# A graph block and a ConvLSTM on one NeuronCore: the scan's x terms partly from memory with shifted taps, 128-row products only, and another place for the load of y

## The chip, the cores and the metric

One NeuronCore of a Trainium2 chip. The metric is the device time of one execution in microseconds (us), the median of three runs. The core has TensorE (PE; its weight loads PEld), VectorE (DVE), ScalarE (ACT), GpSimd (POOL) and SyncE (SP), which issues nearly all DMA transfers here and does them in program order, as every engine does its own list.

## The reference

x is (16, 48, 32, 32). Two blocks follow each other, in float32:

```
# block 1: graph convolution in windows of 8 x 8 nodes
y    = affine(conv1x1(x, fc1))                       # 48 channels
idx  = top_k(-dist(normalized nodes), 9)             # 9 nearest of 64 nodes
feat = [x_i, x_j - x_i];  h = max_k gelu(affine(feat @ ew.T + eb))
x1   = affine(conv1x1(h, fc2)) + x
# block 2: ConvLSTM over the 32 rows of x1, forward and backward, 3 taps along the row
gates = conv1d(concat[x1_row, h], w_mid, 3 taps) + b  # i, f, g, o: 4 x 48 channels
c = sigmoid(f) * c + sigmoid(i) * tanh(g);  h = sigmoid(o) * tanh(c)
y = w_proj @ [h_fwd, h_bwd];  out = relu(batchnorm(y)) + x1
```

## The kernel before, in words

**Graph stage.** The 32 groups (a row of windows of two images, 512 nodes) are worked off in turns 0 to 31, a software pipeline: in turn g, PE gathers the edges of group g with one-hot matrices (line 632), ACT takes the gelu (L849), DVE the maximum over the neighbours (L1242), while DVE makes the one-hot matrices of group g+1 (L1227) from the spread indices `ib` and finds the neighbours of group g+3 (L1210, L1218). Each engine has its own `turn(j, b)`. SP's turn issues, in an order written out by hand: the load of y of group g+3 (`load_y`, L297), the x for the residual (`load_xres`), the store of the indices of group g+3 (`store_idx`, L323), the store of x1, the keys of group g+5 (`load_keys`, L306), and the spread of the indices to 64 partitions each (`spread_idx`, L332), which first waits until the store has landed. From turn 14 on a turn also loads one block of the scan's weights (`load_scan_weight`, L401) and a piece of a mask (`load_rest`, L406). Groups 0 to 7 give rows 0 to 7 of x1, groups 8 to 15 rows 24 to 31, then rows 16 to 23 and 8 to 15. POOL and ACT write x1 to `xh` as two float32r parts: the low part to partitions 0 to 47, the high part to 64 to 111.

**Scan.** 32 steps; in each the forward direction d = 0 (row s), then the backward one d = 1 (row 31−s). A product is taken as high·high + high·low + low·high. Per half-step PE adds 18 products of 512 columns into two PSUM banks (m = 0: gates i and f; m = 1: g and o), three taps each:

- `x_part` (L703): six over `xh`, 128 rows: x low, x high, and in the gaps (partitions 48 to 63 and 112 to 127) two sixteens of x high once more, for the low part of the weights. Copies inside SBUF put them there (`load_twins`, L413).
- `h_part`, first six (L718): 48 rows each, h high in `ht` for m = 0 and in `he` for m = 1, with the low weights `w_e`. These wait for `h_top` (POOL's copy of h, L1119) and `h_edge` (ACT's copy, L920).
- `h_part`, last six (L724): 128 rows of `ht`: h high, a row of ones, h low, and the third sixteen of x high. They wait for `h_lo` (POOL's subtraction, L1121) and for `x_third`, a copy that SP may issue only when the gates of the step before are done (`load_third`, L422).

Then ACT takes two tanh (L904, L910), DVE makes the cell and h (L1335, L1343, L1346, L1353) with a tanh of ACT between (L914), and POOL and ACT write h back in parts. SP stores h to memory (`store_h`, L461), loads x1 for the residual (`load_x1r`), and from step 17 on the h of both directions for the projection, two products on PE per step (`project`, L735). SP, PE, DVE, ACT and POOL run steps in loops: PE, ACT and DVE steps 2 to 13 as two rounds of six steps, SP and POOL most of their steps.

Of the kernel before, what the change touches and what calls it, by code (L numbers as in the profile page):

```python
# [22 lines left out]
P = 128  # L23
# [31 lines left out]
def build(nc, xs, xrow, w1, ones_sel, col1, jcol, wedge, edge_scale, edge_shift, ident9, w2, col2,  # L55
# [5 lines left out]
    x1_d = nc.dram_tensor("x1_d", [H, C, B, W], F32, kind="Internal").ap()  # L61
    hist_d = nc.dram_tensor("hist_d", [H, 2, C, B, W], F32, kind="Internal").ap()

    with ExitStack() as ctx:
# [29 lines left out]
        with ExitStack() as sx:  # L94
            a = sb_in(sx)
            wl_raw = a("wl_raw", [P, 3, 2, 2, TAPS, TOP], F32)
            wl_head = a("wl_head", [P, 2, 2, 2, TAPS, TOP], F32R)
            x1t = a("x1t", [P, 2, HG], F32)
# [6 lines left out]
        rests = sb("rests", [P, 2], F32)  # L105
# [72 lines left out]
        def gate_banks(k, d):  # L178
# [14 lines left out]
            wl_loaded wl_scaled wl_heads wl_split w_e_ready rests_set rests_here gates tanh_if tanh_go cells cells_kept cell_parts tanh_c  # L193
            x_twin00 x_twin01 x_twin10 x_twin11 x_third0 x_third1
# [62 lines left out]
        def _(sp):  # L257
# [129 lines left out]
            for c in range(10, CHUNKS):  # L387
# [5 lines left out]
            scan_rows = ((0, 0, HALF, C), (0, C, HALF, 16), (0, HALF, HALF, C), (0, TOP, HALF + 16, 16),  # L393
                         (1, 0, 0, C + 1), (1, C + 1, C, 1), (1, C + 2, C + 2, 14), (1, HALF, 0, C),
                         (1, TOP, HALF + 32, 16), (2, 0, 0, HALF), (2, HALF, 0, HALF))
            rest_rows = ((0, C, HALF - C), (0, TOP, P - TOP), (1, C + 1, HALF - C - 1), (1, TOP, P - TOP))

            def load_scan_weight(n):

                k, first, src, rows = scan_rows[n]  # L400
                sp.dma_start(wl_raw[first:first + rows, k], wl[src:src + rows]).then_inc(S["wl_loaded"], 16)  # L401

# [6 lines left out]
            def load_twins(s, d, b):  # L409

                row = row_of(s, d)
                for first, src in ((C, HALF), (TOP, HALF + 16)):
                    sp.dma_start(xh[first:first + 16, reg(row, 0, 1), 0:SLOT - 1].bitcast(F32),  # L413
                                 xh[src:src + 16, reg(row, 0, 1), 0:SLOT - 1].bitcast(F32)) \
                        .then_inc(S[f"x_twin{d}{b}"], 16)

            def load_third(s, d):

                if later(s):
                    sp.wait_ge(S["gates"], s * 4 + (2 * d - 2))  # L420
                src = xh[HALF + 32:TOP, reg(row_of(s, d), 0, 1), 0:SLOT - 1].rearrange("p o n -> p (o n)")
                sp.dma_start(ht[TOP:P, d, 0:SLOT - 1].bitcast(F32), src.bitcast(F32)) \  # L422
                    .then_inc(S[f"x_third{d}"], 16)

            def turn(j, b):
                if isinstance(j, int) and nth(j, b, 0)[0] in (GROUPS - 4, GROUPS - 3):
                    d = nth(j, b, 0)[0] - (GROUPS - 4)
                    sp.wait_ge(S["x1_hi"], 2 * PAIRS)
                    sp.wait_ge(S["pads_set"], 9)
                    for s in range(2):  # L430
                        load_twins(s, d, s)
                    load_third(0, d)
                for k, stage in ((3, load_y), (0, load_xres), (3, store_idx), (-2, store_x1), (5, load_keys),
# [3 lines left out]
                if isinstance(j, int) and j > 0:  # L437
# [4 lines left out]
                    if at < len(scan_rows):  # L442
                        load_scan_weight(at)
                    if at < len(rest_rows):
                        load_rest(at)

            for b in range(2):
                turn(0, b)
# [39 lines left out]
            def step(s, b):  # L488
                for d in range(2):
                    if not isinstance(s, int) or s + 1 < H:  # L490
                        load_third(s + 1, d)
                    if isinstance(s, int) and s + 2 < H // 2:
                        load_twins(s + 2, d, b)
                    store_h(s, d)
                    if isinstance(s, int) and 2 <= s < H // 2 + 2:
                        load_x1r(s - 2, d)
                if later(s, H // 2 + 1):
                    load_h(s - 1, 1 - b)

            step(0, 0)  # L500
            store_x1(GROUPS - 1, 1, GROUPS // 2 - 1)
            step(1, 1)
            for b in range(2):
                sp.wait_ge(S[f"x1_stored{b}"], 32 * (GROUPS // 2))
            sp.wait_ge(S["x1_split"], GROUPS)
            sp.dma_start(wp_sb[:], wp).then_inc(S["consts2"], 16)
            sp.dma_start(wp_low[:], wp[C:O]).then_inc(S["consts2"], 16)
            sp.dma_start(gb_sb[:], gb).then_inc(S["consts2"], 16)
            sp.dma_start(comb_sb[:], comb).then_inc(S["consts2"], 16)
            sp.wait_ge(S["w_e_ready"], 1)  # L510
            with sp.Fori(1, H // 4 - 1) as j:
                for b in range(2):
                    s = j * 2 + b
                    for d in range(2):
                        load_third(s + 1, d)
                        load_twins(s + 2, d, b)
                        store_h(s, d)
                        load_x1r(j * 2 + (b - 2), d)
            for s in range(14, 18):
                step(s, s % 2)  # L520
            with sp.Fori(0, H // 4 - 2) as j:
                for b in range(2):
                    step(j * 2 + (18 + b), b)
# [3 lines left out]
            step(30, 0)  # L527
# [11 lines left out]
        def _(pe):  # L539
# [155 lines left out]
            def x_part(s, d, k, n=None):  # L695

                if n is not None:
                    pe.wait_ge(S[f"x_twin{d}{k % 2}"], n * 32 + 32)
                for m in range(2):
                    for t in range(TAPS):  # L700
                        rhs = xh[:, reg(row_of(s, d), 0, 1), t:t + (W + 1) * B] \
                            .rearrange("p o (b w) -> p (o b) w", w=W + 1)[:, :, 0:W]
                        pe.matmul(gate_banks(k, d)[m][0:TOP, :], w_xh[:, 0, d, m, t], rhs, start=(t == 0), stop=False)  # L703

            def h_part(s, d, k):

                if later(s):
                    pe.wait_ge(S["h_top"], s * 2 + (d - 1))
                    pe.wait_ge(S["h_edge"], s * 2 + (d - 1))

                def moving(t, rows, k):
                    return t[rows, d, k:k + (W + 1) * B].rearrange("p (b w) -> p b w", w=W + 1)[:, :, 0:W]

                if later(s):
                    for t in range(TAPS):
                        for m, src in ((0, ht), (1, he)):
                            rows = slice(HALF * m, HALF * m + C)
                            pe.matmul(gate_banks(k, d)[m][0:TOP, :], w_e[rows, d, m, t], moving(src, rows, t),  # L718
                                      start=False, stop=False)
                    pe.wait_ge(S["h_lo"], s * 2 + (d - 1))  # L720
                pe.wait_ge(S[f"x_third{d}"], s * 16 + 16)
# [760 lines left out]
```

## Time and profile before

| what | value |
|---|---|
| median of 3 runs (lowest, highest) | 638.73 us (636.04, 639.83) |
| the profiled execution, and its span | 642.67 us, 640.9 us |
| mean granted TensorE clock | 0.945 |
| busy: PE, DVE, ACT, POOL | 574.0, 500.4, 435.9, 251.7 us |
| bytes read and written in HBM | 48.84 MB, 22.15 MB |

The profile is of one execution. The span runs from its first to its last instruction; the profiled execution's own time stands beside it. Until about 85 us the kernel makes y and the keys, until about 346 us it runs the turns, until 613 us the steps of the scan, then the statistics, the output and the last stores. Rows of the trace give the start from the span's begin and the duration, both in us; "x6" merges six instructions in a row of one kind; what stands in brackets is idle time of the engine before the instruction and who ended it.

### The profile page before, as it was taken

How to read it: one execution, taken by the hardware profiler on the slowest of the kernel's cores; microseconds unless marked ns; L12 is line 12 of the kernel's file. 1: busy time of each engine (PE TensorE's matmuls, PEld its weight loads, DVE VectorE, ACT ScalarE, POOL GpSimd, SP SyncE). 2: the span in 40 equal slices, each digit the busy share in tenths (PEclk: the TensorE clock that was granted, in tenths of full speed). 3: DMA queues.
4: the chain of work that ended last, by engine and by line, in shares of the span. 5: the costliest groups of instructions: out<-in, count | busy, mean ns of one | idle time of the engine just before them, and what ended most of it. 6: DMA issues, size and time to landing. Idle time of an engine off the chain costs nothing.

```text
span 640.9 us, 12616 instructions
## 1 busy us (share of the span) xinstructions
PE 574.0 (90%) x3404; PEld 340.9 (53%) x3404; DVE 500.4 (78%) x962; ACT 435.9 (68%) x645; POOL 251.7 (39%) x299
## 2 busy tenths in 40 slices
PE   6993699999999999979979989999999999999970
PEld 1232366666665556555545656666666556555530
DVE  2687669999999979997998657666667677776765
ACT  3771369999999969877886655555555556565645
POOL 2660004333333323333866634444444434343410
PEclk9996689999999979998997999999999999999985
DMA  8857646655656776777531233333322222222316
GB/s 216 260 148 220 185 118 141 140 141 141 141 142 156 153 146 155 145 137 152 132 76 32 48 82 86 80 79 79 78 64 68 76 77 80 78 67 65 96 55 197
DMA packets 101751, 75.77 MB, mean 118 GB/s; under 512 B 52883, under 2 KB 85141, under 8 KB 101381
## 3 DMA queue, kind: packets, MB, share of 16 engines
q1 hardware_dynamic: 100948, 71.69, 45.3%
q10 hardware_dynamic: 768, 3.67, 2.3%
q8 instruction: 15, 0.25, 0.2%
q14 instruction: 20, 0.16, 0.1%
HBM read 48.84 MB, written 22.15 MB: 111 GB/s over the span
## 4 chain that ended last, share of the span: by engine, by line
PE 47%; DVE 28%; issue 10%; DMA 6%; SPq 3%; ACT 2%; DVEq 1%; POOL 1%; ACTq 0%; POOLq 0%
DVE hmax L1242 11%; PE pz L724 10%; PE pz L703 9%; PE pz L718 5%; DVE onehot L1227 5%; PE p_edge L724 5%; PE p_edge L703 4%; DVE idx L1218 3%; PE p_edge L718 3%; PE pz L554 3%; PE pz L632 2%; DMA idx_d<-idx 2%; DMA y_hl<-y_d 2%; DVE val L1210 2%; PE p_keys L546 1%
## 5 line engine op out<-in xcount | busy, mean ns | idle before, releaser
L1242 DVE TENSOR_REDUCE hmax<-gel 96x128 f32<-96x1024 f32 x128 | 151.7, 1203 | 16.6 <-ACT gel L849 16.6
L849 ACT ACTIVATE gel<-pz 96x1024 f32<-96x1024 f32 x128 | 130.5, 1020 | 37.8 <-PE pz L632 27.6
L1119 POOL CAST ht<-h 48x512 fp32r<-48x512 f32 x62 | 37.5, 605 | 141.9 <-DVE h L1353 141.3
L1121 POOL TENSOR_TENSOR ht<-h,ht 48x512 fp32r<-48x512 f32 x62 | 73.5, 1185 | 5.0
L724 PE MATMUL pz<-ht,w_xh 128*112 128x512 f32 x258 | 71.9, 414 | 1.6 <-DMA ht<-xh 1.6
L703 PE MATMUL pz<-xh,w_xh 128*112 128x512 f32 (+1 forms) x258 | 69.1, 404 | 0.0
L632 PE MATMUL pz<-onehot,ab_hi 64*96 64x512 f32 x256 | 61.3, 475 | 4.0 <-ACT gel L849 3.4
L914 ACT ACTIVATE pz<-c 48x512 f32<-48x512 f32 x43 | 25.7, 597 | 48.0 <-DVE c L1346 48.0
L724 PEld LDWEIGHTS pz<-ht,w_xh 128*112 128x112 f32 x258 | 41.9, 175 | 28.4 <-issue 14.7
L703 PEld LDWEIGHTS pz<-xh,w_xh 128*112 128x112 f32 x258 | 45.7, 178 | 16.8 <-issue 0.7
L632 PE MATMUL pz<-onehot,ab_lo 64*96 64x512 f32 x256 | 53.4, 412 | 0.0
L1353 DVE SCALAR_TENSOR_TENSOR h<-tgo,pz 48x512 f32<-48x512 f32 x43 | 29.7, 690 | 30.2 <-ACT pz L914 30.2
L632 PE MATMUL pz<-ident,ab_lo 64*96 64x512 f32 x256 | 53.1, 410 | 0.0
L632 PE MATMUL pz<-ident,ab_hi 64*96 64x512 f32 x256 | 52.9, 409 | 0.0
L1227 DVE TENSOR_SCALAR onehot<-ib,jcol_sb 128x1024 fp32r<-128x1024 uint16 x64 | 49.0, 767 | 2.3 <-DMA ib<-idx_d 2.3
L1077 POOL TENSOR_TENSOR xh<-x1t,x1c 48x256 f32 (+1 forms) x32 | 34.3, 1072 | 38.0 <-DVE onehot L1227 37.3
L1063 POOL TENSOR_TENSOR x1t<-side,xres 112x256 f32<-112x256 f32 x32 | 24.6, 767 | 56.9 <-ACT side L856 53.2
L1335 DVE SCALAR_TENSOR_TENSOR cu<-pz,c 48x512 f32<-48x512 f32 x43 | 29.9, 694 | 21.4 <-ACT pz L904 21.2
L593 PE MATMUL p_edge<-we_hi,y_hl 97*128 97x192 f32 x128 | 34.1, 302 | 11.3 <-DMA y_hl<-y_d 9.7
L920 ACT ACTIVATE he<-h 48x512 fp32r<-48x512 f32 x62 | 39.1, 631 | 1.6
L718 PE MATMUL pz<-ht,w_e 48*112 48x512 f32 x123 | 38.5, 419 | 1.7 <-ACT he L920 0.8
L718 PE MATMUL pz<-he,w_e 48*112 48x512 f32 x123 | 39.4, 426 | 0.0
(148 smaller groups left out, 1219.3 us busy)
## 6 DMA issues: line engine op xcount, KB each, us to landing
ib<-idx_d SPq DMA_DIRECT2D x64, 256.0 KB, 4.3
y_d<-y SPq DMA_DIRECT2D x32, 192.0 KB, 3.3
y_hl<-y_d SPq DMA_DIRECT2D x32, 192.0 KB, 4.1
hist_d<-h SPq DMA_DIRECT2D x62, 96.0 KB, 1.9
hp<-hist_d SPq DMA_DIRECT2D x30, 192.0 KB, 2.7
kr<-xn_d SPq DMA_DIRECT2D x32, 98.0 KB
xn_d<-x_in SPq DMA_DIRECT2D x32, 96.0 KB, 2.3
kl<-xn_d SPq DMA_DIRECT2D x32, 96.0 KB
```

Source lines behind the costliest of these rows:

```text
L593: pe.matmul(o, lhs, we_hi[0:O + 1, 0:2].rearrange("p a o -> p (a o)"), start=(t % 2 == 0), stop=False, skip_group_check=True)
L632: mm = pe.matmul(pz[0:O, 2 * (t % 2) + s, :], part[rows, b, t, which], moving[rows], start=(n == 0), stop=(n == 3))
L703: pe.matmul(gate_banks(k, d)[m][0:TOP, :], w_xh[:, 0, d, m, t], rhs, start=(t == 0), stop=False)
L718: pe.matmul(gate_banks(k, d)[m][0:TOP, :], w_e[rows, d, m, t], moving(src, rows, t), start=False, stop=False)
L724: mm = pe.matmul(gate_banks(k, d)[m][0:TOP, :], w_xh[:, 1, d, m, t], moving(ht, slice(0, P), t), start=False, stop=(t == TAPS - 1))
L849: act.activation(gel[:, t % 2], pz[0:O, 2 * (t % 2):2 * (t % 2) + 2, :], ACT.Gelu) \
L920: act.activation(h_slots(he, HALF, d), h2[0:C, d].rearrange("p (b w) -> p b w", w=W), ACT.Copy) \
L1077: pool.tensor_tensor(slots(0, g)[:, 0], by_row(x1t[0:C, b]), by_row(x1c[0:C]).bitcast(F32), ALU.subtract).then_inc(S["x1_half"], 1)
L1119: pool.tensor_copy(h_slots(ht, 0, d), columns(h2[0:C, d])).then_inc(S["h_top"], 1)
L1121: pool.tensor_tensor(h_slots(ht, HALF, d), columns(h2[0:C, d]), h_slots(ht, 0, d).bitcast(F32), ALU.subtract).then_inc(S["h_lo"], 1)
L1227: dve.tensor_scalar(onehot[:, b, 2 * half:2 * half + 2], ib[:, b, 2 * half:2 * half + 2], jcol_sb[:, 0:1], None, ALU.is_equal).then_inc(S[ ...
L1242: dve.tensor_reduce(dst, gel[:, t % 2].rearrange("p w (r c k) -> p w r c k", r=WS, k=KN), AX_X, ALU.max).then_inc(S["maxed"], 1)
```

## The change

**Scan.** The products per half-step become 14, in three groups. `x_part` is two products (one for each m) over `xt`, 98 rows: the lowest 32 channels of x low, three times, shifted by 0, 1 and 2 columns, and two rows of ones for the bias. They come from a new array in memory, `xl_d`, in one load whose pattern overlaps itself, two steps ahead. `h_part` begins with six products over `xh`, whose partitions 0 to 47 now hold the high part of h: POOL writes it there for the next step's row, over x low, which has been stored to `xl_d` before. Its last six go over `ht`: h low, 16 channels of x low, h high (ACT's copy), and 16 channels of x high, the two sixteens loaded from `xl_d` for every step. `he`, `w_e` and the short products are gone; `w_xh` becomes `w_rows`, `w_x` is new. Weights: two blocks in place of three, and five small loads for the taps.

**Preparation.** In turns 14 to 21 and 26 to 29 and in steps 2 to 5, SP stores the low part and 16 channels of the high part of two rows of x1 to `xl_d` and copies the twins of these rows; per pair of rows, four transfers. **Graph stage.** `load_y` stands for group g+4 between `load_keys` and `spread_idx`, no longer for group g+3 at the front. **Programs.** SP's, PE's and POOL's steps are written out in place of loops; DVE's and ACT's blocks keep theirs. At row 16, which both directions have used by then, POOL waits once for the gates of both.

```
-    w_xh = sb("w_xh", [P, 2, 2, 2, TAPS, TOP], F32R)
-    w_e = sb("w_e", [P, 2, 2, TAPS, TOP], F32R)
+    w_rows = sb("w_rows", [P, 2, 2, 2, TAPS, TOP], F32R)
+    w_x = sb("w_x", [P, 2, 2, TOP], F32R)
-    he = sb("he", [P, 2, SLOT], F32R)
+    xt = sb("xt", [P, 2, 2, SLOT], F32R)
...
+    def store_lows(r, sem):
+        for first, rows, src in ((0, C, 0), (C, HALF - C, HALF + 32)):
+            sp.dma_start(xl_d[r:r + 2, first:first + rows].rearrange("r c n -> c r n"),
+                         xh[src:src + rows, r:r + 2, 0:SLOT - 1].bitcast(F32)).then_inc(S[sem], 16)
...
+    def load_twins(r, sem):
     for first, src in ((C, HALF), (TOP, HALF + 16)):
+        sp.dma_start(xh[first:first + 16, r:r + 2, 0:SLOT - 1].bitcast(F32),
+                     xh[src:src + 16, r:r + 2, 0:SLOT - 1].bitcast(F32)).then_inc(S[sem], 16)
...
+    def load_shifts(s, d):
+        lows = xl_d[row_of(s, d), 0:32, 0:SLOT - TAPS]
+        sp.dma_start(xt[0:96, d, s % 2, 0:SLOT - TAPS].bitcast(F32),
+                     bass.AP(lows.tensor, lows.offset, [[1, TAPS], [SLOT - 1, 32], [1, SLOT - TAPS]])) \
+            .then_inc(S[f"x_shifts{d}{s % 2}"], 16)
...
-    for k, stage in ((3, load_y), (0, load_xres), (3, store_idx), (-2, store_x1), (5, load_keys),
+    for k, stage in ((0, load_xres), (3, store_idx), (-2, store_x1), (5, load_keys), (4, load_y),
                      (3, spread_idx)):
...
+        if at < 8:
+            block, part = divmod(at, 4)
+            sp.wait_ge(S["x1_split"], PAIRS * (block + 1))
+            store_lows((0, 24)[block] + 2 * part, "xl_stored0")
+            load_twins((0, 24)[block] + 2 * part, "x_twins0")
...
+    for d in range(2):                                    # SP, step(s)
+        if s + 1 < H:
+            sp.wait_ge(S["gates"], s * 4 + (2 * d + 2))
+            load_thirds(s + 1, d)
+        if s + 2 < H:
+            load_shifts(s + 2, d)
+        store_h(s, d)
...
+    def h_part(s, d, k):                                  # PE
+        if later(s):
+            pe.wait_ge(S["h_top"], s * 2 + (d - 1))
+        for m in range(2):
+            for t in range(TAPS):
+                row = xh[:, reg(row_of(s, d), 0, 1), t:t + (W + 1) * B].rearrange("p o n -> p (o n)")
+                pe.matmul(gate_banks(k, d)[m][0:TOP, :], w_rows[:, 0, d, m, t], by_column(row),
+                          start=False, stop=False)
+        pe.wait_ge(S[f"x_third{d}"], s * 32 + 32)
...
-    pool.tensor_copy(h_slots(ht, 0, d), columns(h2[0:C, d])).then_inc(S["h_top"], 1)
+    if s == H // 2 - 1 and d == 0:
+        pool.wait_ge(S["gates"], 4 * (s + 1))
+    head = xh[0:C, reg(row_of(s + 1, d), 0, 1), 1:1 + (W + 1) * B] \
+        .rearrange("p o (b w) -> p (o b) w", w=W + 1)[:, :, 0:W]
+    pool.tensor_copy(head, columns(h2[0:C, d])).then_inc(S["h_top"], 1)
```

PE, one half-step of the scan before (`w_xh` and `w_e` are the weights; of the six products over `xh`, which register work parts into three rows, the last row is shown):

```order
L703 MATMUL pz<-xh,w_xh 112x512 x4
L718 MATMUL pz<-ht,w_e 112x512
L718 MATMUL pz<-he,w_e 112x512
L718 MATMUL pz<-ht,w_e 112x512
L718 MATMUL pz<-he,w_e 112x512
L718 MATMUL pz<-ht,w_e 112x512
L718 MATMUL pz<-he,w_e 112x512
L724 MATMUL pz<-ht,w_xh 112x512 x6
```

and now, a step and the first group of the next (line numbers of the changed kernel):

```order
L728 MATMUL pz<-xt,w_x 112x512 x2
L738 MATMUL pz<-xh,w_rows 112x512 x6
L746 MATMUL pz<-ht,w_rows 112x512 x6
L728 MATMUL pz<-xt,w_x 112x512 x2
L738 MATMUL pz<-xh,w_rows 112x512 x6
L746 MATMUL pz<-ht,w_rows 112x512 x6
L728 MATMUL p_edge<-xt,w_x 112x512 x2
```

Six products over `xh` and six short ones per half-step became two over `xt` and six over `xh`, and those over `xh` moved behind the wait for h's head.

SP, a turn of the graph stage with a block of weights, before:

```order
L332 DMA ib<-idx_d 64x4x512 x2
L401 DMA wl_raw<-wl 49x1344
L297 DMA y_hl<-y_d 96x2x256
L316 DMA xres<-xrow 48x256 x2
L323 DMA idx_d<-idx 128x4x8
L342 DMA x_d<-x1t 48x8x32 x2
L306 DMA kl<-xn_d 48x2x256
L306 DMA kr<-xn_d 49x2x256
```

and now, from one spread of the indices (`ib`) to the next:

```order
L335 DMA ib<-idx_d 64x4x512 x2
L404 DMA wl_raw<-wl 48x1344
L414 DMA xl_d<-xh 48x2x529
L414 DMA xl_d<-xh 16x2x529
L426 DMA xh<-xh 16x2x529 x2
L319 DMA xres<-xrow 48x256 x2
L326 DMA idx_d<-idx 128x4x8
L345 DMA x_d<-x1t 48x8x32 x2
L309 DMA kl<-xn_d 48x2x256
L309 DMA kr<-xn_d 49x2x256
L300 DMA y_hl<-y_d 96x2x256
```

The load of y moved from behind the weights to behind the keys, and the two stores to `xl_d` and the two copies of twins stand between the weights and the next store of the indices.

SP, one step of the scan now (before, a half-step had one copy to `ht`, two to `xh`, the store of h and one row for the residual):

```order
L439 DMA ht<-xl_d 16x529 x2
L432 DMA xt<-xl_d 96x1x527
L493 DMA hist_d<-h 48x512
L517 DMA x1r<-x_d 64x512
L439 DMA ht<-xl_d 16x529 x2
L432 DMA xt<-xl_d 96x1x527
L493 DMA hist_d<-h 48x512
L511 DMA x1r<-x_d 48x512
```

Each half-step has two loads of sixteens and one load of 96 shifted rows, all from memory.

## Rows read from the trace of the kernel before

**Rows 1.** Busy time by stretch: the engines' us, granted clock, DMA share, GB/s.
```profile
core 0: us, PE busy (x) PEld busy (x) DVE busy (x) ACT busy (x) POOL busy (x), PEclk, DMA share, GB/s
100.00:150.00 50.00, 48.15 (x429) 31.01 (x426) 49.34 (x125) 46.41 (x64) 19.28 (x26) 1.00 0.60 142
200.00:250.00 50.00, 46.90 (x386) 29.79 (x385) 46.19 (x113) 42.73 (x60) 17.81 (x24) 0.93 0.74 154
250.00:300.00 50.00, 45.21 (x363) 28.60 (x363) 43.91 (x104) 40.31 (x57) 16.02 (x22) 0.93 0.74 152
360.00:400.00 40.00, 37.64 (x172) 23.77 (x172) 26.11 (x38) 22.40 (x38) 18.42 (x22) 1.00 0.27 71
```

**Rows 2.** Chain of waits, one half-step of the scan: start, us, what.
```profile
429.34 1.43 PE pz L703 x6
...
430.86 0.95 PE pz L718 x6
431.82 1.60 PE pz L724 x6
```

**Rows 3.** Chain of waits: third pieces of steps 3, 13, 16, 19, 30; a projection.
```profile
375.13 1.59 PE pz L724 x6
...
456.13 1.59 PE pz L724 x6
...
480.16 1.60 PE pz L724 x6
...
505.61 1.59 PE pz L724 x6
...
544.39 1.01 PE p_out L735 x4
...
603.96 1.59 PE pz L724 x6
```

**Rows 4.** Timeline of step 15, direction 0.
```profile
468.06 1.69 PE L724 MATMUL pz<-ht,w_xh 128*112 128x512 f32 x6
...
472.56 0.69 DVE L1353 SCALAR_TENSOR_TENSOR h<-tgo,pz 48x512 f32<-48x512 f32 x1 [0.66 <-ACT pz L914]
...
473.42 0.60 POOL L1119 CAST ht<-h 48x512 fp32r<-48x512 f32 x1 [2.13 <-DVE h L1353]
...
474.10 1.18 POOL L1121 TENSOR_TENSOR ht<-h,ht 48x512 fp32r<-48x512 f32 x1
```

**Rows 5.** Timeline: h of a step inside DVE's loop.
```profile
432.55 0.69 DVE L1353 SCALAR_TENSOR_TENSOR h<-tgo,p_edge 48x512 f32<-48x512 f32 x1 [0.97 <-ACT p_edge L914]
```

**Rows 6.** Chain of waits, start of step 3.
```profile
368.99 1.93 DMA ht<-xh
```

**Rows 7.** Timeline of SP in the scan: two copies of twins.
```profile
419.68 1.26 SPq L413 DMA_DIRECT2D xh<-xh  x2
```

**Rows 8.** Timeline of DVE: first one-hot product of two turns.
```profile
152.97 0.74 DVE L1227 TENSOR_SCALAR onehot<-ib,jcol_sb 128x1024 fp32r<-128x1024 uint16 x1
...
160.92 0.74 DVE L1227 TENSOR_SCALAR onehot<-ib,jcol_sb 128x1024 fp32r<-128x1024 uint16 x1
```

**Rows 9.** Timeline of SP: a turn without weight loads, one with.
```profile
149.04 0.43 SPq L323 DMA_DIRECT2D idx_d<-idx  x1
...
152.09 1.47 SPq L332 DMA_DIRECT2D ib<-idx_d  x2
...
217.97 1.28 SPq L332 DMA_DIRECT2D ib<-idx_d  x2
...
220.40 0.38 SPq L297 DMA_DIRECT2D y_hl<-y_d  x1
...
221.78 0.43 SPq L323 DMA_DIRECT2D idx_d<-idx  x1
...
227.17 1.27 SPq L332 DMA_DIRECT2D ib<-idx_d  x2
```

**Rows 10.** Timeline of PE: a wait for y.
```profile
225.16 0.36 PE L593 MATMUL p_edge<-we_hi,y_hl 97*128 97x192 f32 x1 [1.41 <-DMA y_hl<-y_d]
```

**Rows 11.** DMA issues: KB each, median us from issue to landing.
```profile
ib<-idx_d SPq DMA_DIRECT2D x64, 256.0 KB, 4.3
```

More of the change, by code:

```diff
@@ L407, in load_rest, with load_thirds @@
                              allow_slow_non_contiguous=True).then_inc(S["rests_here"], 16)
-            def load_twins(s, d, b):
-                row = row_of(s, d)
+            def load_twins(r, sem):
                 for first, src in ((C, HALF), (TOP, HALF + 16)):
[L413 to L423, printed above, removed]
+                    sp.dma_start(xh[first:first + 16, r:r + 2, 0:SLOT - 1].bitcast(F32),
[5 more added lines that the diff above has]
+                    .then_inc(S[f"x_shifts{d}{s % 2}"], 16)
+            def load_thirds(s, d):
+                for q in range(2):
+                    sp.dma_start(ht[HALF * q + C:HALF * q + HALF, d, 0:SLOT - 1].bitcast(F32),
+                                 xl_d[row_of(s, d), 32 + 16 * q:C + 16 * q]).then_inc(S[f"x_third{d}"], 16)
             def turn(j, b):
@@ L486, in load_x1r, with step @@
                                  x1_rows[reg(i * C, (H // 2) * C, HALF)]).then_inc(S["x1r_loaded"], 16)
-            def step(s, b):
+            def step(s):
                 for d in range(2):
[L490 to L493, printed above, removed]
-                    store_h(s, d)
[L495 to L498, printed above, removed]
@@ L503, in _ @@
+                if s >= H // 2 + 1:
+                    load_h(s - 1, 1 - s % 2)
+            step(0)
+            store_x1(GROUPS - 1, 1, GROUPS // 2 - 1)
+            step(1)
+            sp.wait_ge(S["x1_split"], GROUPS)
+            for s in range(2, 6):
+                step(s)
+            sp.wait_ge(S["xl_stored1"], 32 * 8)
             for b in range(2):
                 sp.wait_ge(S[f"x1_stored{b}"], 32 * (GROUPS // 2))
-            sp.wait_ge(S["x1_split"], GROUPS)
-            sp.dma_start(wp_sb[:], wp).then_inc(S["consts2"], 16)
@@ L507, in _ @@
[L507 to L523, printed above, removed]
+            consts = ((wp_sb[:], wp), (wp_low[:], wp[C:O]), (gb_sb[:], gb), (comb_sb[:], comb))
+            for s in range(6, 30):
+                step(s)
+                if s < 10:
+                    dst, src = consts[s - 6]
+                    sp.dma_start(dst, src).then_inc(S["consts2"], 16)
@@ L526, in _ @@
                     .then_inc(S["first_loaded"], 16)
-            step(30, 0)
+            step(30)
             load_h(30, 0)
@@ L691, in _, with by_column, x_part @@
             turns(pe, turn)
[L695 to L698 removed]
+            def by_column(t):
+                return t.rearrange("p (b w) -> p b w", w=W + 1)[:, :, 0:W]
+            def x_part(s, d, k):
+                pe.wait_ge(S[f"x_shifts{d}{s % 2}"], s // 2 * 16 + 16)
                 for m in range(2):
[L700 to L703, printed above, removed]
+                    pe.matmul(gate_banks(k, d)[m][0:TOP, :], w_x[0:98, d, m], by_column(xt[0:98, d, s % 2, 0:(W + 1) * B]),
+                              start=True, stop=False)
             def h_part(s, d, k):
```

168 lines of the change are left out of this document (92 added, 76 removed).

## The prediction

> **What bounds the kernel now.** I read the windows first, because the two stages have different limits. In the graph stage (100 to 150 us) DVE is busy 49.34 of 50 us and a turn cannot be shorter; between 200 and 300 us DVE falls to 46.19 and 43.91 of 50 us and the granted clock to 0.93, so that stretch loses 2 × 49.34 − 46.19 − 43.91 = 8.6 us against an undisturbed one [rows 1]. In the scan PE takes over: the chain of waits consists there of PE alone, in pieces that repeat every half-step: six products over xh 1.43 us, six short ones over ht and he 0.95 us, six over ht 1.60 us, and waits below 0.1 us between them [rows 2]. The starts of the third piece of direction 1 in steps 3, 13, 16, 19 and 30 give the step: 81.00 us / 10 = 8.10 us in the part that DVE, ACT and PE run as a loop, 24.03 / 3 = 8.01 us just behind it, and 98.35 / 11 = 8.94 us where the projection (1.01 us on PE) comes in once a step [rows 3].
>
> **The scan, PE's side.** A half-step loses six products over xh with 128 rows and the six short ones, and gains two products over xt (98 rows) and six over xh with the new weights. The last six stay. That leaves 14 products where there were 18, twelve of which filled PE alone. A product over 128 rows takes 1.43 / 6 = 0.238 us [rows 2]; the 98-row product streams the same 512 columns, so I give it the same price. A half-step of PE is then 14 × 0.238 = 3.33 us, a step 6.67 us. If PE stayed the bound, a step would be about 7.1 us with four waits of 0.1 us.
>
> **The scan, the loop through one direction.** It does not stay the bound everywhere. In step 15 the last six products start at 468.06, h is made at 472.56, POOL writes its head from 473.42 to 474.02 and its low part from 474.10 to 475.28 [rows 4]. Before, six short products (0.95 us) wait for the head and the last six for the low part. Now six full products wait for the head: 474.02 + 0.1 + 1.43 = 475.55, and the last six start at once behind them; the low part (475.28) is there earlier, and so is ACT's copy of h, for which the short products waited already. So a direction cannot turn faster than 475.55 − 468.06 = 7.49 us, say 7.5. In the loop DVE starts h in every other half-step 0.97 us after its last work and not 0.66 [rows 5]; DVE's block keeps its loop, so steps 2 to 13 get 7.5 + 0.31 = 7.8 us. In the steps with the projection PE needs 6.67 + 1.01 + 0.3 for waits = 7.98 us, more than 7.5, so PE bounds them again.
>
> Sum over rows 3: 10 × (8.10 − 7.80) = 3.0; 3 × (8.01 − 7.50) = 1.5; the 25.45 us from step 16 to 19 are two steps of 8.01, one of 8.94 and 0.5 that DVE spends on the constants once, which becomes 2 × 7.5 + 7.98 + 0.5 = 23.5, gain 1.95; 11 × (8.94 − 7.98) = 10.6; step 31 gives 0.96. Together **18.0 us**. I leave the first three steps at nothing: step 0 has 14 products instead of 12 in a half-step (about 1 us lost), the short pieces of steps 1 and 2 fall away, and the load of a third that SP could only issue after the last x1 was split, 1.93 us on the chain [rows 6], is late again, since SP still waits for that split and then has two loads to issue. Bounds 2 us to either side. The crossing in step 15, where POOL now waits for both directions' gates before it overwrites row 16, costs nothing: the gates of direction 1 end 3.75 + 1.7 us after the start of direction 0's last six, h of direction 0 at 4.5 + 0.7 us.
>
> **What SP has to do for it.** Per half-step it now issues two thirds, one shifted load of 96 rows, the store of h and one row for the residual: five issues at no more than 0.63 us each (half of the 1.26 us of two such copies) [rows 7], 3.2 of 3.75 us. SP is held by the store of h, 5.2 us after the start of direction 0's last six; the store and the residual row bring it to 6.4, two thirds to 7.6, and the second lands 1.93 us [rows 6] after its issue at 7.0, so at 8.9; direction 1's last six need it at 3.75 + 7.5 = 11.2. Cover 2.3 us, and beyond it each us late is one us a step. The shifted taps are loaded two steps (15 us) ahead. The queue's share was 0.27 here [rows 1]: room enough. The POOL product for w_e, the smaller scalings and the unrolled programs lie beside DVE's or PE's work; nothing for them.
>
> **The graph stage.** A turn of DVE is 160.92 − 152.97 = 7.95 us [rows 8]. SP's own circle is: spread of the indices, weight load, y, two xres, store of the next indices, wait until it landed, spread. Undisturbed the store lands in 3.05 us (149.04 to 152.09), and the circle waits for DVE. With a weight load in it the circle took 227.17 − 217.97 = 9.20 us, 3.81 of issue and 5.39 for the landing [rows 9], so SP fell behind, and y came late: PE waited 1.41 us at 225.16 [rows 10] and lost some clock too. The change puts y in front of the spread, into the time in which SP waits for the landing anyway. So y comes some 4 us earlier, its wait ends, and 0.38 us leave the circle. It adds, in turns 14 to 21 and 26 to 29, four transfers of 404 KB together: two stores of the lows, two copies of the twins. At 0.63 us each that is 2.5 us of issue in the circle. Lower bound: 3.81 − 0.38 + 2.5 + 3.05 = 8.98 us, if the queue is empty when the indices are stored. Upper bound: 3.81 − 0.38 + 2.5 + 5.39 = 11.3 us, if they find the queue as full as before. I take 9.2: the bytes that delayed the store have 2.1 us more to drain, and y is no longer among them. Over eight turns that is 8 × (9.2 − 7.95) = 10.0 us behind DVE. DVE has a lead to lose first: the spread issued at 152.09 is used at 160.92; 0.74 for the first issue and 4.3 to landing [rows 11] leave 3.8 us, less 0.7 for y's bytes in front. The stage then loses 10.0 − 3.1 = 6.9 us instead of 8.6: gain **1.7 us**; bounds: gain 4.2 (8 × 1.03 − 3.8 = 4.4 lost), loss 15.1 (8 × 3.35 − 3.1 = 23.7 lost). Turns 26 to 29 have no weight load, so less than 8.98 us each: at most 4 us behind in four turns, against the lead of 3.1; nothing for them.
>
> The rows show an index store landing 5.39 us after its issue with a weight block in front, 3.05 without. The Trainium skill (DMA: Bandwidth & Descriptors, section Queues, rings and completion order) says that a semaphore's increment lands only after every earlier write of its DMA engine, which speaks against these stores: taken strictly, 404 KB at the stretch's 154 GB/s, 2.6 us (an estimate), would stand behind the 8.82 us that are left of the circle, 11.4 us, and the kernel would end near 637. The trace agrees with the order of landing, but it shows the queue half empty for much of a turn (share 0.74 [rows 1]), so I keep 9.2.
>
> **Sum.** 18.0 + 1.7 = 19.7 us. The profiled execution took 642.67 us (span 640.9 and 1.8 around it), 3.9 more than the median of the runs, 638.73; its steps are those of any run, so 642.67 − 19.7 = 623.0 for it and **619.0 us** for the median.
>
> **Rivals.**
> 1. *Slower: the circle of SP in the graph stage.* If lows and twins cost issue and queue time in full, DVE waits for ib in every turn from 15 on. The kernel ends above 641.9 us when the stage loses 18.0 + 3.2 us more than now, so 29.8 + 3.1 = 8 × (C − 7.95), C = 12.1 us. At 12.6 us (the upper bound and two issues that take twice as long): 8 × 4.65 − 3.1 = 34.1 lost, 25.5 more than now, 638.7 − 18.0 + 25.5 = 646 us. For it: circles of 9.2 us already. Against: the upper bound is 11.3. Chance 0.06.
> 2. *The scan keeps its step*, because the thirds, now two loads from memory behind 202 KB of shifted taps, arrive 2.3 us later than reckoned and more. Only the graph stage gains: 637 us. For it: a third was on the chain once [rows 6]; against: the cover. Chance 0.10, with circles of 11.3 to 12.1 us counted here (636 to 642).
> 3. *The clock.* With a step bound by the loop, PE stands still 7.5 − 6.67 = 0.8 us a step. If that dropped it from 2.4 to 1.2 GHz, a half-step would take 6.67 us and a step 13.3: 29 steps × 5 us more, about 780 us. Against: from 360 to 400 us PE was busy 37.64 of 40 us, with a wait of nearly 2 us in it, at a clock of 1.00 [rows 1, 6]. The Trainium skill (TensorE: Matmul & The Clock Gate, section A second HAM failure mode) tells of a kernel whose short pauses between groups of matmuls made the clock go up and down. Chance 0.02.
>
> **How the numbers follow.** Forecast 0.82. Low end: 18.0 + 4.2, the register wait gone (13 × 0.3 = 4), 2 us at the start and 2.7 of spread (636.04 below 638.73): 638.7 − 30.9 = 608. High end: 638.7 − 18.0 + 15.1 = 635.8, so 636. No change is what lies within 0.5% (3.2 us, about what a measurement can tell). Faster 0.82; same 0.10; slower 0.06 + 0.02.
>
> **What would show it.** Right: steps of 7.8, 7.5 and 8.0 us between starts of the last six products; POOL's head on the chain of waits before step 18, PE alone behind it; no wait of PE for y; DVE waits of 5 to 9 us in all for ib between 215 and 285 us; issues of the spread 9 us apart in turns 14 to 21. Wrong: waits of PE for ht or xt from memory in the scan, circles over 10 us, a clock below 1.00 in the scan.

## The result, and the profile after it

The change made the kernel slower: 648.65 us (median of 4 runs, 643.39 to 650.59) against 638.73, ratio 1.0155 with a 95% interval of 1.0106 to 1.0204. The forecast was 619.0, range 608 to 636, so it failed in sign and in size. The profiled execution took 646.94 us, 1.7 below its median, where that of before stood 3.9 above its own; between the two executions the difference is 4.3 us, and that is what the rows have to account for. The other 5.6 us of the 9.9 between the medians lie between executions, and no row here shows them. One execution of a later kernel (e9 below) took 2719 us where its three others took 615 to 620; it is left out of that kernel's numbers.

I laid the starts of the last six products of direction 0 side by side (line 724 before, 746 after) and cut the span at steps 0, 17 and 31. Steps 17 and 31, first in the kernel before and then in the changed one ("step 19" below is the time from this start in step 18 to that in step 19):

```profile
484.10 1.68 PE L724 MATMUL pz<-ht,w_xh 128*112 128x512 f32 x6
608.81 1.69 PE L724 MATMUL p_edge<-ht,w_xh 128*112 128x512 f32 x6
481.57 1.58 PE L746 MATMUL pz<-ht,w_rows 128*112 128x512 f32 x6
613.00 1.58 PE L746 MATMUL p_edge<-ht,w_rows 128*112 128x512 f32 x6
```

| stretch | before | after | change | forecast |
|---|---|---|---|---|
| up to step 0 (graph stage) | 345.75 | 348.25 | +2.5 | -1.7 |
| step 0 to 17 | 138.35 | 133.32 | -5.0 | -5.0 |
| step 17 to 31 | 124.71 | 131.44 | +6.7 | -13.0 |
| after that | 32.05 | 31.89 | -0.2 | 0 |

The forecast column is the prediction's own sum cut at the same places. The second stretch came out at the forecast sum (by luck in part, see below). Nearly all of the miss, 19.7 of 23.9 us, lies in the steps with a projection; 4.2 lie in the graph stage.

First the windows of the changed kernel, the stretches of [rows 1] (same columns) and one over the late steps:

```profile
200.00:250.00 50.00, 42.69 (x378) 27.11 (x377) 45.78 (x113) 42.59 (x58) 16.07 (x23) 1.00 0.81 182
250.00:300.00 50.00, 46.11 (x372) 29.40 (x372) 44.18 (x104) 41.25 (x57) 14.32 (x22) 0.93 0.79 168
360.00:400.00 40.00, 34.13 (x133) 22.07 (x132) 26.15 (x38) 23.50 (x41) 18.93 (x23) 1.00 0.46 123
484.00:545.00 61.00, 51.55 (x191) 32.58 (x190) 36.71 (x56) 30.84 (x53) 22.30 (x25) 0.92 0.47 136
```

DVE, which should be busy 49.3 of 50 us, still loses 3.6 and 5.2 us in the graph stage. In the late scan the DMA share is 0.47: by that number half of the DMA engines' time is free. PE was busy for 51.55 of its 61 us, and the granted clock was 0.92.

What PE stood still for is in the chain of waits of 484 to 545 us (start, us, what):

```profile
492.99 5.93 DMA hp<-hist_d
498.96 1.98 PE p_keys L757 x4
500.94 2.83 PE p_edge L738 x6
...
514.95 4.86 DMA hp<-hist_d
...
533.56 4.96 DMA hp<-hist_d
```

The projection waits for hp, the rows of h that come back from memory. DMA hp is 25.8% of that stretch of the chain, and its loads were not in the prediction's list of what SP has to do. It costs twice: behind the first wait six products take 2.83 us that take 1.67 elsewhere, and step 19 takes 13.26 us in place of 8.9. SP did not issue hp late: its first load went out at 492.65, right behind a residual row, and PE wanted it at 495.88. Its second load landed 5.93 us after its issue; the first thirteen times this took 3.5 to 7.0 us, and before 2.5 to 3.4.

Why it lands late shows in the list of DMA issues (KB each, median us from issue to landing; a row without the last number has no landing that could be matched):

```profile
xt<-xl_d SPq DMA_DIRECT2D x64, 197.6 KB
hist_d<-h SPq DMA_DIRECT2D x62, 96.0 KB, 4.8
hp<-hist_d SPq DMA_DIRECT2D x30, 192.0 KB, 3.3
ht<-xl_d SPq DMA_DIRECT2D x128, 33.1 KB, 2.9
x1r<-x_d SPq DMA_DIRECT2D x15, 128.0 KB, 5.0
```

The same rows of the kernel before:

```profile
hist_d<-h SPq DMA_DIRECT2D x62, 96.0 KB, 1.9
hp<-hist_d SPq DMA_DIRECT2D x30, 192.0 KB, 2.7
x1r<-x_d SPq DMA_DIRECT2D x15, 128.0 KB, 2.6
```

The store of h, unchanged in size, lands after 4.8 us; before it took 1.9. Its landings (the steps in which its semaphore counts up) are more telling than the median: of the 16 of a store issued at 491.63, thirteen come from 493.09 to 493.54, on time, and three from 497.09 to 497.31. So most of the 16 DMA engines are free and three are far behind. The shifted load is the odd one: each of its 64 issues shows 4 landings where every other transfer of the scan shows 16, and its packets (2108 bytes, found by their size) run 2.8 at a time on average between 480 and 500 us. That gave the theory for the experiments: the load is cut along its outermost dimension, the three taps, and fills three engines.

### The profile page after: what moved, and what is told of

Its sections match the earlier page's. It is cut to its first block, busy times and chain, and to the rows that moved or that the text cites. A ratio compares the mean times of both kernels' runs of the same rounds, so it can differ in the third digit from the quotient of the medians.

```text
span 644.9 us, 11504 instructions
## 1 busy us (share of the span) xinstructions
PE 549.8 (85%) x3160; PEld 333.0 (52%) x3160; DVE 500.1 (78%) x963; ACT 437.1 (68%) x645; POOL 242.5 (38%) x299
## 2 busy tenths in 40 slices
DMA packets 112517, 94.72 MB, mean 147 GB/s; under 512 B 54560, under 2 KB 86818, under 8 KB 112146
## 4 chain that ended last, share of the span: by engine, by line
DVE 31%; PE 19%; DMA 15%; issue 12%; SPq 12%; ACT 7%; POOL 2%; DVEq 1%; POOLq 0%; ACTq 0%
DVE hmax L1272 8%; DMA hp<-hist_d 5%; PE pz L738 4%; DVE onehot L1257 4%; DVE c L1381 3%; DVE cu L1370 3%; DMA idx_d<-idx 3%; PE pz L580 3%; DVE idx L1248 3%; PE p_edge L738 2%; DVE h L1388 2%; PE pz L746 2%; DMA x_d<-x1t 2%; SPq L426 2%; DVE pz L1378 2%
## 5 line engine op out<-in xcount | busy, mean ns | idle before, releaser
L1155 POOL CAST xh<-h 48x512 fp32r<-48x512 f32 x62 | 37.6, 606 | 145.3 <-DVE h L1388 143.1
L738 PE MATMUL pz<-xh,w_rows 128*112 128x512 f32 x258 | 72.2, 416 | 5.9 <-POOL xh L1155 5.7
L1157 POOL TENSOR_TENSOR ht<-h,xh 48x512 fp32r<-48x512 f32 x62 | 73.6, 1186 | 5.0
L746 PE MATMUL pz<-ht,w_rows 128*112 128x512 f32 x258 | 69.3, 404 | 3.7 <-DMA ht<-xl_d 3.7
L738 PEld LDWEIGHTS pz<-xh,w_rows 128*112 128x112 f32 x258 | 43.2, 178 | 35.3 <-POOL xh L1155 17.3
L746 PEld LDWEIGHTS pz<-ht,w_rows 128*112 128x112 f32 x258 | 44.8, 177 | 22.6 <-DMA ht<-xl_d 7.6
L1257 DVE TENSOR_SCALAR onehot<-ib,jcol_sb 128x1024 fp32r<-128x1024 uint16 x64 | 48.1, 753 | 10.3 <-DMA ib<-idx_d 10.2
L606 PE MATMUL p_keys<-kr,kl 128*64 128x64 f32 x512 | 23.2, 236 | 22.1 <-DVE idx L1248 11.1
L942 ACT ACTIVATE ht<-h 48x512 fp32r<-48x512 f32 x62 | 39.2, 632 | 1.5
L658 PEld LDWEIGHTS pz<-onehot,ab_hi 64*96 64x96 f32 x256 | 21.4, 162 | 33.1 <-issue 22.9
L738 PE MATMUL p_edge<-xh,w_rows 128*112 128x512 f32 x126 | 36.2, 424 | 2.3 <-POOL xh L1155 2.0
```

The costliest lines, as they stand in the source:

```text
L658: mm = pe.matmul(pz[0:O, 2 * (t % 2) + s, :], part[rows, b, t, which], moving[rows], start=(n == 0), stop=(n == 3))
L738: pe.matmul(gate_banks(k, d)[m][0:TOP, :], w_rows[:, 0, d, m, t], by_column(row), start=False, stop=False)
L746: mm = pe.matmul(gate_banks(k, d)[m][0:TOP, :], w_rows[:, 1, d, m, t], by_column(ht[:, d, t:t + (W + 1) * B]), start=False, stop=(t == TAP ...
L942: act.activation(h_slots(ht, HALF, d), h2[0:C, d].rearrange("p (b w) -> p b w", w=W), ACT.Copy) \
L1155: pool.tensor_copy(head, columns(h2[0:C, d])).then_inc(S["h_top"], 1)
L1157: pool.tensor_tensor(h_slots(ht, 0, d), columns(h2[0:C, d]), head.bitcast(F32), ALU.subtract).then_inc(S["h_lo"], 1)
```

## The experiments

Each kernel is compared with runs of the kernel before on the same chip. Stage ends (the start of step 0's last six products) and steps are from each one's profiled execution; a turn is taken from the start of DVE's first maximum to that of the next.

**One load in another order (e1).** The rival is that the change moves too many bytes, wherever they run: 94.72 MB in all against 75.77, of which the shifted loads are 64 × 96 rows of 2108 bytes, 13.0 MB (the 18 MB in the expectation are about the whole increase, 19, and not this load).

```
-                dst = wx_raw[first:first + rows]
+                dst = wx_raw[t:96:TAPS] if rows == 32 else wx_raw[first:first + rows]
...
-   bass.AP(lows.tensor, lows.offset, [[1, TAPS], [SLOT - 1, 32], [1, SLOT - TAPS]])
+   bass.AP(lows.tensor, lows.offset, [[SLOT - 1, 32], [1, TAPS], [1, SLOT - TAPS]])
```

> The changed kernel, but the shifted load (L432) walks the 32 rows of x1 first and the three taps inside (the rows of its weights are put in the same order): same bytes, same number of DMAs, another order. In the changed kernel each shifted load shows 4 landings where every other load shows 16, its 96 packets of 2108 bytes run about 3 at a time, and the history store, first landing after 1.5 us, lands last after 4.8 us. Theory A (the shifted load is cut into three lists, one for each tap, which fill three of the 16 DMA engines, and whatever else is queued on those three comes late): now 16 landings a load, the history store back at 1.9 to 2.5 us, no wait of TensorE for hp, step (17,0) to (31,0) down from 131.4 to 110 to 114 us (the 112 of the prediction's terms), time 626 to 634. Theory B (the load's 18 MB as such make the others late, by whichever engines): landings of the history store stay over 4 us, waits for hp stay, time 643 to 652.

Measured: 629.51 us, ratio 0.9804 (0.9751 to 0.9856). From step 17 to 31 117.0 us against 131.4. The same bytes are now 16 landings a load (256 in place of 64 on each of the four semaphores), 10 packets at a time between 480 and 500 us, and the list of issues reads

```profile
xt<-xl_d SPq DMA_DIRECT2D x64, 197.6 KB, 2.9
hist_d<-h SPq DMA_DIRECT2D x62, 96.0 KB, 1.9
hp<-hist_d SPq DMA_DIRECT2D x30, 192.0 KB, 2.8
ht<-xl_d SPq DMA_DIRECT2D x128, 33.1 KB, 2.0
x1r<-x_d SPq DMA_DIRECT2D x15, 128.0 KB, 2.8
```

The window over the late steps, with the clock back at 1.00 and a **higher** DMA share than in the slow kernel:

```profile
484.00:545.00 61.00, 57.87 (x230) 35.95 (x230) 44.56 (x68) 38.18 (x65) 25.77 (x30) 1.00 0.54 150
```

Theory A holds and B falls: with the same volume the loss is gone, so the volume's place on the engines was the fault. Two parts of the expectation did not come out. The stretch is 117.0 us and not 110 to 114, and a few waits for hp remain (from 484 to 545 us 0.4 us of PE's products, where the changed kernel has 7.9). The Trainium skill (DMA: Bandwidth & Descriptors, section Why a DMA increments its semaphore by 16 and not by 1) states that a transfer runs on the largest number of engines up to 16 that divides the slowest dimension on both sides, and that the engines which it leaves out are counted at once. For 3 taps and 96 partitions that is 3, and 4 landings; for 32 rows and 96 partitions it is 16. The traces agree with both, 4 landings a load in the changed kernel and 16 in e1.

**Is it only hp's place in SP's order (e8)?**

```
                     if s + 2 < H:
                         load_shifts(s + 2, d)
+                    if d == 0 and s >= H // 2 + 1:
+                        load_h(s - 1, 1 - s % 2)
                     store_h(s, d)
...
-                if s >= H // 2 + 1:
-                    load_h(s - 1, 1 - s % 2)
```

> The changed kernel, its shifted load as it was (three taps outermost), with the load of hp half a step earlier. A second rival to theory A: the projection waits only because hp stands too far back in SP's order. Then this edit alone takes the steps with a projection to 8.0 to 8.4 us, time 634 to 641. By theory A the history store still lands after 4.8 us, SP then waits for it in front of hp with the loads of the next thirds behind it, and the time stays within 645 to 655.

Measured: 643.14 us, ratio 1.0077 (1.0035 to 1.0119), between the two expectations. The store still lands after 4.8 us, and SP stands in front of hp as theory A has it: behind the shifted load that ends at 505.79 nothing is issued until 508.71 (the store issued at 503.20, for which hp waits, has thirteen landings by 505.02 and the last three from 508.15 to 508.63), so the store of h, the residual row and the next thirds are late in turn: from 484 to 545 us no product of PE waits for hp, and 4.6 us are waits for thirds.

```profile
505.10 0.69 SPq L432 DMA_DIRECT2D xt<-xl_d  x1
508.71 0.78 SPq L503 DMA_DIRECT2D hp<-hist_d  x2
509.54 0.42 SPq L493 DMA_DIRECT2D hist_d<-h  x1
```

But the stretch from 17 to 31 fell from 131.4 to 121.8 us, more than A allowed. So hp's place is worth 9.7 us while three engines are filled, and the load's order 14.4 without a change of place. The lateness has one cause, the three engines; how dear it is depends on how little room hp was given.

**The load of y alone (e2)**, in the kernel before:

```
-  for k, stage in ((3, load_y), (0, load_xres), (3, store_idx), (-2, store_x1), (5, load_keys),
+  for k, stage in ((0, load_xres), (3, store_idx), (-2, store_x1), (5, load_keys), (4, load_y),
                    (3, spread_idx)):
...
+            load_y(3, 1, 1)
             for b in range(2):
                 turn(0, b)
```

> The kernel before with one part of the change: the load of y one turn earlier and in front of the spread of the indices. Theory C (in the kernel before the late y is what stretches the turns in which SP also loads weights): no wait of the edge products for y is left, the graph stage ends up to 8.6 us earlier, time 630 to 634. Rival D (the turns' length is SP's circle from spread to spread, which the order of the loads doesn't shorten): waits for y go, waits of VectorE for the indices take their place, time 636 to 640.

Measured: 632.17 us, ratio 0.9856 (0.9808 to 0.9904). Turns 18 to 26 of DVE take 7.95 us, where before turn 18 took 11.39 and turn 25 13.59; no wait of PE for y is left. DVE in its windows:

```profile
200.00:250.00 50.00, 48.13 (x415) 30.60 (x414) 49.22 (x117) 45.58 (x64) 18.76 (x25) 1.00 0.81 156
250.00:300.00 50.00, 46.93 (x405) 29.95 (x406) 47.40 (x115) 45.14 (x63) 19.08 (x28) 1.00 0.82 158
```

Theory C holds: 8.4 us between the medians. The window 200 to 250 has the same share of 0.81 as the changed kernel's and loses 0.1 us and not 3.6: this share, too, says little of who waits.

**y back in its old place (e3)**, in the changed kernel (the same edit reversed).

> The changed kernel with the load of y back in its old place, first in the turn. Theory C: waits for y come back in the twelve turns with low parts and twins, the circle of some 9.5 us stays, the graph stage ends 2 to 6 us later than in the changed kernel, time 651 to 655. Rival D: the circle alone counts, time within 2 us of 648.7.

Measured: 660.31 us, ratio 1.0302 (1.0240 to 1.0364), more than either theory gave. Waits for y come back (14.0 us of PE's weight loads, 9.9 of its products, 190 to 300 us), and the stage ends 12.1 us later than in the changed kernel. The medians are 11.7 us apart, so the move of y is worth no less with low parts and twins in the turns than without.

**Fewer, larger low parts and twins (e4)**, in the changed kernel.

```
-                    if at < 8:
...
+                    if at in (0, 4, 12):
+                        sp.wait_ge(S["x1_split"], PAIRS * (at // 4 + 1 - at // 12))
+                        first = {0: 0, 4: 24, 12: 16}[at]
+                        store_lows(first, f"xl_stored{at // 12}", 8)
+                        load_twins(first, f"x_twins{at // 12}", 8)
```

> The changed kernel with the same low parts and twins written in the graph stage, 8 rows at a time in three turns (4 DMAs each) in place of 2 rows at a time in twelve turns (48 DMAs). SP then issues 36 DMAs less, some 0.5 us each, the bytes are the same. Theory E (the circle of SP, in issued DMAs, stretches the turns): the nine turns that lose their four DMAs fall from about 9.1 us to 8.0 to 8.3, the graph stage ends 6 to 10 us earlier, time 639 to 643, the scan as in the changed kernel. Rival F (the bytes in flight make the spread of the indices land late): the turns with a bundle grow by what the others lose, time within 3 us of 648.7.

Measured: 663.76 us, ratio 1.0332 (1.0263 to 1.0400). Theory E falls, and the time lies 12 us above rival F's range too. The turns without a bundle did fall (7.95 us in turns 18 to 24 but for turn 21), but turns 17 and 21, which have one, take 16.54 and 17.26 us, 17.9 above 7.95 together, where the changed kernel's turns 18 to 24 lose 9.75 for the same rows. SP's row of the first bundle:

```profile
203.33 0.93 SPq L414 DMA_DIRECT2D xl_d<-xh  x2
204.30 6.78 SPq L426 DMA_DIRECT2D xh<-xh  x2
211.13 4.15 SPq L319 DMA_DIRECT2D xres<-xrow  x2
```

Two copies of twins that take 1.34 us to issue as 2 rows take 6.78 as 8 rows, with all of SP's queue behind them. So the count of issues is not the price. F named the bytes in flight, and what the row shows is SP held while it issues. Spread thin, these transfers cost less than in a lump: 9.75 us in the changed kernel, and 12.4 to 16.6 in the same turns of e8, e5 and e1.

**hp earlier, on top of e1 (e5)** (the edit of the second experiment).

> The kernel of e1 (rows first in the shifted load) with the load of hp issued half a step earlier, in front of the store of h for d = 0. In e1 the steps from 21 on take 8.2 to 8.5 us against 7.98 of the prediction, and in five of eight such steps the projection waits up to 0.5 us for hp, which SP issues about 3 us before it is wanted. If that wait sets the step: steps 21 to 31 at 7.9 to 8.1, 3 to 5 us less than e1, time 624 to 627. If ScalarE's extra copy of the projection (line keep) and the row of VectorE set it: within 1.5 us of e1.

Measured: 631.07 us, ratio 0.9859 (0.9800 to 0.9919). Steps 21 to 31 take 8.36 us on average in both. The remaining waits for hp were not what set the step: once the three engines are free, hp's place costs nothing that can be seen.

**Low parts and twins in the scan**, on top of e1 (e6), and both together (e7):

```
-                    if at < 8:
...
-                    if 12 <= at < 16:
...
+                    if at in (1, 3, 5, 7):
...
-                    if 2 <= s < 6:
-                        (store_lows, load_twins)[d](4 + 2 * s, ("xl_stored1", "x_twins1")[d])
+                    if s < 12:
+                        (store_lows, load_twins)[d](27 - s if s % 2 else 4 + s, ("xl_stored", "x_twins")[d] + str(1 + s // 2 % 2))
```

> The kernel of e1 with the low parts and twins of rows 4 to 27 written in the first twelve steps of the scan in place of the graph stage (only rows 0 to 3 and 28 to 31 stay there, in four turns that are not neighbours), and the loads of x1r six steps later. Theory G (the low parts and twins are what makes the changed kernel's graph stage long, by the bytes and SP's time they take in front of the indices): the turns fall to 7.95 but for those four, the graph stage ends 8 to 13 us earlier than in e1, the scan's first steps grow by 0 to 4 us, time 616 to 623. Rival H (the early steps of the scan can't take four more transfers a step: SP or the DMA engines make the thirds late): steps 2 to 12 at 8.3 us or more in place of 7.7, time 623 to 632.

> e5 and e6 in one kernel. If both hold and are independent: 612 to 619; if only the low parts and twins count: 616 to 623.

Measured: 625.19 us (0.9786, 0.9745 to 0.9827) and 623.06 us (0.9758, 0.9719 to 0.9797). In the profiles the graph stage of e6 ends 10.3 us earlier than in e1, and that of e7 8.2 earlier than in e5, as theory G has it. In e6 steps 2 to 12 stay at 7.6 to 8.0 but for step 3 (8.25); rival H falls. The medians moved less than the profiles, for e1's profiled execution (635.02) was its slowest run: the ratios of e1 and e6 differ by 0.2%, well within their intervals. Between e5 and e7, which differ by this edit alone, the intervals just lie apart, 1.0% or 6.4 us. The times stand 2 us (e6) and 4 us (e7, if both edits had paid) above their ranges, since hp earlier brought nothing and steps 21 to 31 still take 8.40 us (e6) and 8.36 us (e7). What sets them shows in the chain of e7:

```profile
559.80 0.70 DVE c L1384
560.53 0.22 ACT pz L939
560.75 0.40 issue
561.15 0.60 ACT y_sb L950
561.77 0.58 ACT pz L929
562.38 0.70 DVE cu L1373
```

ACT's copy of the projected row (y_sb, keep) stands between the cell's tanh of direction 0 and the gates' tanh of direction 1, on the loop.

**keep in ACT's idle time (e9)**, on top of e7:

```
                     if more:
                         h_edge(*prev)
+                    if d == 0 and later(s, H // 2 + 3) and isinstance(s, int):
+                        i = s - (H // 2 + 3)
+                        keep(i, i % 2)
...
-                    if d == 0 and later(s, H // 2 + 3) and isinstance(s, int):
...
```

> The kernel of e7 with ScalarE's copy of the projected row (keep) behind h_edge and in front of the cell's tanh of d = 0, where ScalarE is idle for over 1 us, in place of behind that tanh, where it stands 0.6 us in front of the tanh of the gates for d = 1. If this copy is what is left of the steps with a projection (8.38 in e7 against 7.98 of the prediction): steps 21 to 31 at 7.8 to 8.1, 3 to 6 us less than e7, time 617 to 620. If VectorE's or TensorE's own work sets the step: within 1 us of e7.

Measured: 616.07 us (median of three executions), ratio 0.9669 (0.9588 to 0.9750). Steps 21 to 31: 8.05 us, as expected if the copy set them. The copy now lies in a gap of 1.5 us, as the timeline of ACT in e10, which has the same edit, shows:

```profile
548.90 0.63 ACT L945 ACTIVATE ht<-h 48x512 fp32r<-48x512 f32 x1
549.56 0.60 ACT L950 ACTIVATE y_sb<-p_keys 128x512 f32<-128x512 f32 x1
551.08 0.60 ACT L939 ACTIVATE pz<-c 48x512 f32<-48x512 f32 x1 [0.92 <-DVE c L1384]
```

**The last four pieces in turns without weight loads (e10)**, on top of e9:

```
-                    if at in (1, 3, 5, 7):
+                    if at in (-2, -1, 11, 12):
```

> The kernel of e9 with the four pieces of low parts and twins that are left in the graph stage moved from the turns that also load weights (18, 20, 22 and 24 by VectorE's count, 9.1 to 10.8 us in e7) to turns 15 and 16, ahead of the weights, and 28 and 29, behind them. If a piece costs what SP's circle has no room for: turns 18 to 24 at 7.95, 15 and 16 at 8.0 to 9.5, 28 and 29 as they were, 4 to 8 us less than e9. If a piece costs its bytes wherever it stands: within 2 us of e9.

Measured: **613.00 us**, ratio 0.9606 (0.9544 to 0.9668), the best kernel here. That is 3.1 us less than e9, a little under what was expected, and the two intervals overlap: the times alone do not tell the two apart. The turns do. Turns 15 to 25 all take 7.95 or 7.96 us, so in turns 15 and 16 a piece (the four transfers of a pair of rows) costs nothing, where in turns 18, 20, 22 and 24 it cost 1.2 to 2.9 us in e7 and 0 to 2.5 in e9. Its windows, to be read against [rows 1]:

```profile
200.00:250.00 50.00, 48.09 (x418) 30.09 (x416) 49.34 (x121) 45.78 (x64) 19.00 (x25) 1.00 0.84 165
250.00:300.00 50.00, 47.96 (x422) 30.61 (x419) 49.33 (x125) 45.34 (x63) 22.11 (x33) 1.00 0.78 159
```

DVE is back at 49.3 of 50 us, at a DMA share like that of the changed kernel, which lost 3.6 and 5.2 us there.

## Why the prediction was wrong

**The failed step: "The queue's share was 0.27 here [rows 1]: room enough."** It took the mean share of 16 engines as the room for a transfer. The change's shifted load puts 96 packets on three engines, 32 each. At 0.086 us a packet (the median; the mean is 0.106 between 480 and 500 us) that is 2.75 to 3.4 us of a half-step of 3.8. Every other transfer of the scan shows 16 landings, and for the store shown above three of them came 3.6 us behind the others. So the store of h landed 2.9 us later, the second load of hp up to 7.0 us after its issue, and the projection waited. Steps 17 to 31 took 131.4 us in place of 111.7; with the load spread, 117.0 (e1), and with keep moved too, 113.2 (e9).

**"In the steps with the projection PE needs 6.67 + 1.01 + 0.3 = 7.98 us."** With everything in time 8.36 was measured (e5) and not 7.98. PE was not the bound: the loop over ACT and DVE was, with keep's 0.60 us on it between two tanh. The prediction counted what the projection costs PE and not what it costs ACT. With keep out of the way it is 8.05 (e9), and PE is busy for 84.87 of the 85 us from 500 to 585 in e10: the term itself was right to 0.1 us.

**The loop through one direction** was right. One turn of it in the changed kernel:

```profile
444.02 1.58 PE L746 MATMUL pz<-ht,w_rows 128*112 128x512 f32 x6
...
448.70 0.69 DVE L1388 SCALAR_TENSOR_TENSOR h<-tgo,pz 48x512 f32<-48x512 f32 x1 [0.86 <-ACT pz L936]
...
449.46 0.61 POOL L1155 CAST xh<-h 48x512 fp32r<-48x512 f32 x1 [2.12 <-DVE h L1388]
...
450.12 1.67 PE L738 MATMUL p_edge<-xh,w_rows 128*112 128x512 f32 x6 [0.33 <-POOL xh L1155]
...
451.62 1.58 PE L746 MATMUL p_edge<-ht,w_rows 128*112 128x512 f32 x6
```

From last six to last six 7.60 us: h, POOL's head, six full products, and the last six at once behind them. Steps 7 to 13 took 7.69 on average (7.8 forecast) and 15 to 17 7.44 (7.5). That the gain to step 17 is 5.0 us, as forecast, is luck: two errors cancel. The first three steps, put at nothing, gained 1.9, and step 4, put at a gain of 0.3, lost 1.8. PE waits 2.50 us there for a third. In e1, with the same transfers and only the shifted load spread, step 4 takes 7.74 us and not 9.94, so this is the three engines again.

**The graph stage.** The circle was well reckoned; its small error, times eight, is most of what turns 18 to 24 lost beyond the forecast. Three spreads of the indices in the changed kernel:

```profile
209.08 1.34 SPq L335 DMA_DIRECT2D ib<-idx_d  x2
...
214.99 0.42 SPq L326 DMA_DIRECT2D idx_d<-idx  x1
...
217.83 1.33 SPq L335 DMA_DIRECT2D ib<-idx_d  x2
...
228.25 1.33 SPq L335 DMA_DIRECT2D ib<-idx_d  x2
```

8.75 and 10.42 us; the mean of eight is 9.54, against 9.2, as foreseen with no wait for y and with waits of DVE for ib (7.4 us from 200 to 290). Put into the prediction's own sum, 9.54 gives 8 × 1.59 − 3.1 = 9.6 us. Turns 14 to 30 take 12.2 us longer than in e10, and not 6.9: 9.7 in turns 18 to 24, where e10 loses nothing, and 2.4 in the last five, whose pieces the prediction put at "nothing". Part of the first number may be the clock: in turn 22 PE had waited 1.71 us for keys, and 6 us of half clock followed (below). The kernel before loses 10.0 in the same count, not 8.6. The move of y alone gained 8.4 us by the medians (e2); the transfers put into the same turns took it back. How much they take varies: e1, e5 and e8 have the same turns as the changed kernel, and their stages end 2.1 to 9.5 us later than its.

**The rivals.** Rival 1 named the circle, but a circle of 12.1 us was not needed to be slower, since the scan's gain, which it took as safe, was gone. Rival 2 had loads from memory come late in the scan, by the right mechanism's neighbour: it looked at the thirds, which have a cover of 2.3 us and lost 1 us of it (2.9 in place of 1.9), and not at hp, which PE wants 3.2 us after its issue and which took 2.7 to land in the kernel before. Rival 3's steady half clock did not come; from 360 to 482 us the clock was 1.00.

## What to carry to other kernels

Before a transfer is added, ask on how many DMA engines its pattern lets it run, and judge the room on those: count its landings, or find its packets by their size and see how many run at once (here 4 and 2.8, against 16 and 10). A mean DMA share below one half is no cover where one transfer fills three engines of 16, and the one that suffers is another, the one whose consumer has the least slack. When an engine is freed, list what every other engine does in that step: here the 0.6 us of a copy on ACT became the bound that PE's saved products left behind.

## What the runs showed of the hardware that was not expected

- Three engines, as above: 4 landings and 2.8 packets at a time with three taps outermost, 16 and 10 with 32 rows outermost, at equal bytes.
- The clock. In the changed kernel some waits of PE are followed by a stretch at the lower of the two levels (1.2 GHz), the granted clock by window being

```profile
250.00:258.00 8.00, 6.61 (x50) 4.00 (x48) 7.24 (x19) 6.86 (x10) 2.43 (x4) 1.00 0.77 187
260.00:266.00 6.00, 6.00 (x27) 3.79 (x28) 3.96 (x12) 2.77 (x6) 0.77 (x2) 0.50 0.97 180
490.00:498.00 8.00, 5.89 (x24) 3.79 (x23) 5.80 (x9) 5.12 (x9) 3.57 (x4) 1.00 0.59 155
499.00:505.00 6.00, 6.00 (x14) 3.28 (x15) 0.01 (x1) 0.00 (x0) 1.77 (x2) 0.50 0.46 149
```

  Each came soon after PE, having waited 1.71 us for keys and 3.08 us for hp, took up work again; full clock was back by 270 and 506 us. That a late transfer is paid a second time this way was in no term of the sum. Which waits do it was not tried: the wait of 2.50 us in step 4 was followed by none.
- SP itself stands still when large copies within SBUF are issued: 2.8 to 3.5 us for one instruction with 8 rows (e4), 0.67 with 2 rows. Whether the row length, the 16 partitions or the number of packets does it stays open.
